# An attention layer gated by an FFN on one core: rotary tables kept on chip, one copy of the keys, query jobs per head, heads that take turns

## What is computed

```python
xn = _layernorm(x)
# attention: H=16 heads, NOPE=128, ROPE=64, VD=128, LORA=64
q = (xn @ wq).reshape(b, s, H, 192).transpose(0, 2, 1, 3)
q_nope, q_pe = q[..., :128], q[..., 128:]
kva = xn @ wkv_a;  ckv, k_pe = kva[..., :64], kva[..., 64:]
ckv = ckv * rsqrt(mean(ckv * ckv) + EPS) * kv_norm_scale
k_nope, v = split((ckv @ wkv_b).reshape(b, s, H, 256)...)
q_pe, k_pe = _rope(q_pe, cos, sin), _rope(k_pe, cos, sin)
scores = (q_nope . k_nope + q_pe . k_pe) * 192 ** -0.5    # causal
out = softmax(scores) @ v;   s = out.reshape(b, s, H * 128) @ wo
# FFN: hidden 704
g = silu((silu(xn @ gate_w.T * gate_s) * (xn @ up_w.T * up_s)) @ down_w.T * down_s)
return x + s * g
```

## Time and profile before

| | before |
|---|---|
| runs | 1116.97, 1118.76, 1122.3 us |
| profiled execution | 1120.68 us, its span 1118.9 us |
| TensorE busy | 985.6 us, 88% (10576 matmuls), mean granted clock 0.95 |
| DVE / ACT / GpSimd busy | 831.2 / 714.0 / 662.8 us |
| DMA | 184.92 MB, mean 165 GB/s; SP's queue q1 has 89.6% of 16 engines' span |
| chain that ended last | TensorE 34%, DMA 24%, DVE 17%, GpSimd 10%, SP queue 6%, ACT 5% |

### The profile page before, as it was taken

How to read it: one execution, slowest core, us unless ns; L and a number is a source line. 1 busy time by engine, 2 the same in 40 slices (tenths; PEclk the granted TensorE clock), 3 DMA queues, 4 the chain that set the end, 5 groups by cost and what they waited for, 6 DMA issues and landing times.

```text
span 1118.9 us, 26420 instructions
## 1 busy us (share of the span) xinstructions
PE 985.6 (88%) x10576; PEld 842.8 (75%) x10576; DVE 831.2 (74%) x1359; ACT 714.0 (64%) x1033; POOL 662.8 (59%) x448
## 2 busy tenths in 40 slices
PE   6864898989988988999889998998899986989998
PEld 5743787778777877788778877876688775878887
DVE  6674687988787877878798779887888885873134
ACT  1335567776676767677677677776677774863232
POOL 3736766766576675756685658565857684422331
PEclk7777899999999999899999999999999998999999
DMA  5118899999999999999999999999999899992001
GB/s 146 38 40 168 152 186 197 197 197 184 184 187 199 189 187 185 202 184 188 189 207 185 197 190 206 180 192 178 202 178 211 179 192 207 178 176 76 1 20 57
DMA packets 600042, 184.92 MB, mean 165 GB/s; under 512 B 574960, under 2 KB 586864, under 8 KB 599920
## 3 DMA queue, kind: packets, MB, share of 16 engines
q1 hardware_dynamic: 595440, 182.57, 89.6%
...
## 4 chain that ended last, share of the span: by engine, by line
PE 34%; DMA 24%; DVE 17%; POOL 10%; SPq 6%; ACT 5%; issue 4%; ACTq 1%; POOLq 0%
DMA pT<-hl 19%; PE s_ps L637 12%; PE s_ps L535 9%; DVE hl L948 5%; PE slot_ps L535 5%; DVE part_max L939 5%; POOL hl L1099 5%; ACT hl L743 3%; DMA sinT<-sinT_dram 2%; SPq L464 2%; ACT prob L809 2%; PE o_ps L653 2%; SPq L477 2%; PE o_ps L535 2%; PE o_ps L654 2%
## 5 line engine op out<-in xcount | busy, mean ns | idle before, releaser
L1099 POOL TENSOR_TENSOR hl<-prob,hl 128x1024 f16<-128x1024 f32 x128 | 274.5, 2144 | 228.3 <-ACT hl L743 224.4
L743 ACT ACTIVATE hl<-prob 128x1024 f16<-128x1024 f32 (+7 forms) x384 | 295.9, 804 | 160.3 <-DMA pT<-hl 159.6
L809 ACT ACTIVATE prob<-s_ps,neg_max 128x1024 f32<-128x1024 f32 (+7 forms) x384 | 316.7, 859 | 101.4 <-DVE neg_max L942 46.6
L939 DVE TENSOR_REDUCE part_max<-s_ps 128x1 f32<-128x1024 f32 (+7 forms) x256 | 243.7, 985 | 93.4 <-PE s_ps L637 74.4
L948 DVE TENSOR_TENSOR hl<-prob,hl 128x1024 f16<-128x1024 f32 (+7 forms) x256 | 255.9, 1035 | 62.4 <-ACT hl L743 62.1
L653 PE MATMUL o_ps<-v,pT 128*128 128x65 f16 x2176 | 231.8, 194 | 51.0 <-DMA pT<-hl 39.3
L653 PEld LDWEIGHTS o_ps<-v,pT 128*128 128x128 f16 x2176 | 205.4, 97 | 58.0 <-DMA pT<-hl 45.9
L654 PE MATMUL o_ps<-v,pT 128*128 128x64 f16 x2176 | 232.2, 196 | 0.0
L655 PE MATMUL o_ps<-v,pT 128*128 128x65 f16 x2176 | 231.1, 193 | 0.0
L655 PEld LDWEIGHTS o_ps<-v,pT 128*128 128x128 f16 x2176 | 205.6, 100 | 0.0
L654 PEld LDWEIGHTS o_ps<-v,pT 128*128 128x128 f16 x2176 | 204.8, 98 | 0.0
...
## 6 DMA issues: line engine op xcount, KB each, us to landing
...
q_swap<-q_pe SPq DMA_DIRECT2D x128, 64.0 KB, 2.1
pT<-hl SPq DMA_TRANSPOSE x256, 5.2
...
```

Of the source, the lines that this page charges most:

```text
L743: return nc.scalar.activation(dst, src, ACT.Copy)
L809: nc.scalar.activation(prob_of(u, m), score_bank(u, m), ACT.Exp, bias=neg_max[:, r:r + 1]).then_inc(exp_done, 1)
L939: nc.vector.tensor_reduce(part_max[:, u % 2, m:m + 1], src, AX.X, ALU.max).then_inc(part_done, 1)
L1099: return lambda: nc.gpsimd.tensor_tensor(dst, a, b, op)
```

## The change

1. **Tables.** `cosT` and `sinT` hold all 2048 columns and are loaded once, in the setup, group by group (8 loads in place of 64). `TABLES_AT` and its waits are gone.
2. **One copy of the keys.** Both heads keep rotary rows at partitions 0 to 63, latent rows at 64 to 127. `KB` and its four setup jobs, ACT copies and DVE subtractions are gone.
3. **Query jobs per head.** `qA{g}` and `qB{g}` make all 128 rows of one head. Each has two ACT copies over 64 rows (into `q_pe` and into the query) and one DVE subtraction. The swap waits for `qB{g}`. Head B's sum now moves from partitions 64 to 127 down to 0 to 63: DVE does it (`rope_of_b`, into `pe_b`), GpSimd only head A's.
4. **Heads take turns.** Unit u is head u % 2, and two units in a row have the same tiles. Groups 3 and 0 are due at units 0 and 1 of a pair, groups 2 and 1 at units 8 and 9; the job and step tables are rewritten for it. `o_pair` becomes two buffers of four tiles, the output jobs come sooner and five, not nine, are left for the FFN stage. The FFN loads move from unit 5 to 6, their first use from unit 6 to 8.

The swap is made by four DMAs before and after; only its place moves.

```diff
-    k = u % HALF
+    k = step_of(u)
-    return u // HALF % 2
+    return u % 2
-    k = u % HALF
+    k = step_of(u)
...
-               ("wkvT", 0), ("xT", 3, 0), ("xT", 3, 1), ("pe3", 0), ("kv", 2), ("wabs", 0), ("kv", 3), ("K", 0, "B"), ("K", 0, "A"),
-               ("pe0", 0), ("lat3", 0), ("K", 1, "B"), ("K", 1, "A"), ("lat0", 0), ("K", 2, "B"), ("K", 2, "A"),
-               ("K", 3, "B"), ("K", 3, "A")]
+               ("wkvT", 0), ("xT", 3, 0), ("xT", 3, 1), ("kv", 2), ("wabs", 0), ("kv", 3), ("qA3", 0), ("qB3", 0), ("K", 0), ("K", 1),
+               ("qA0", 0), ("K", 2), ("qB0", 0), ("K", 3)]
...
-JOBS_NEXT = {2: ["wqT"], 5: ["pe3"], 7: ["wkvT"], 8: ["pe0"], 9: ["wabs"], 11: ["pe2", "lat3"], 12: ["lat0"], 13: ["pe1"],
+JOBS_BEFORE = {2: ["outT3"], 4: ["outP3a", "outP3b"]}
+JOBS_OWN = {0: ["qA2"], 1: ["qB2"], 2: ["qA1"], 3: ["qB1"], 5: ["wvo"], 6: ["outT0"], 7: ["outP0a", "outP0b"], 10: ["outT1"],
+            12: ["outP1a", "outP1b"], 14: ["outT2"], 15: ["outP2a", "outP2b"]}
+JOBS_NEXT = {3: ["wqT"], 5: ["wkvT"], 6: ["wabs"], 8: ["qA3"], 9: ["qB3"], 10: ["qA0"], 11: ["qB0"]}
+FFN_COUNT = {8: 1, 9: 2, 10: 1, 11: 2, 13: 2, 14: 1, 15: 2}
+OUT_LAST = [(name, PAIRS - 1) for name in ("outP2a", "outP2b", "outT3", "outP3a", "outP3b")]
...
+POOL_NEXT = {1: ["wkvs"], 6: ["wpe_hi"], 7: ["wpe_lo"], 10: rope(3)[:1], 11: rope(3)[1:] + ["A3hi"], 12: ["A3lo", rope(0)[0], "B3hi"],
+             13: ["B3lo"] + rope(0)[1:], 14: side("A", 0), 15: side("B", 0)}
+POOL_OWN = {2: rope(2)[:1], 3: rope(2)[1:] + ["A2hi"], 4: ["A2lo", rope(1)[0], "B2hi"], 5: ["B2lo"] + rope(1)[1:], 6: side("A", 1),
+            7: side("B", 1)}
+POOL_FFN = {6: ["up_zero", "up_scale_zero", "down_zero"], 8: ["up_scaled0", "up_scaled1"], 9: ["down_scaled"]}
+ROPE_B_OWN, ROPE_B_NEXT = {4: 2, 6: 1}, {12: 3, 14: 0}
...
-    return scores_through((pair - 1) * PU + head * HALF + (HALF // 2 if g in (3, 0) else HALF) - 1)
+    return scores_through((pair - 1) * PU + (PU // 2 if g in (3, 0) else PU) - 2 + head)
...
-        cosT = ab("cosT", [P, BANK])
-        sinT = ab("sinT", [P, BANK])
+        cosT = ab("cosT", [P, S])
+        sinT = ab("sinT", [P, S])
+        pe_b = ab("pe_b", [LORA, 2, BANK])
...
-            def load_tables(g, pair):
-                n = group_no(g, pair)
-                if n >= 1:
-                    before = GROUP_ORDER[(n - 1) % NG], (n - 1) // NG
-                    sp.wait_ge(pool_done, POOL.after((f"rope{before[0]}.1", before[1])))
-                sp.dma_start(cosT[:], cosT_in[:, query_cols(g)]).then_inc(tables_loaded, 16)
-                sp.dma_start(sinT[:], sinT_in[:, query_cols(g)]).then_inc(tables_loaded, 16)
+            def load_tables(g):
+                sp.dma_start(cosT[:, query_cols(g)], cosT_in[:, query_cols(g)]).then_inc(tables_loaded[g], 16)
+                sp.dma_start(sinT[:, query_cols(g)], sinT_in[:, query_cols(g)]).then_inc(tables_loaded[g], 16)
             def swap(g, pair):
                 half = ROPE // 2
-                sp.wait_ge(act_freed, after("act", (f"pe{g}", pair)))
+                sp.wait_ge(hi_done, after("hi", (f"qB{g}", pair)))
                 n = group_no(g, pair)
                 if n >= 1:
                     before = GROUP_ORDER[(n - 1) % NG], (n - 1) // NG
                     sp.wait_ge(pool_done, POOL.after((f"rope{before[0]}.2", before[1])))
+                    sp.wait_ge(rope_b, n)
                 for i in range(4):
...
-                if u in TABLES_AT:
-                    load_tables(*TABLES_AT[u])
                 turn_rest(u)
...
-                if pair == PAIRS - 1 and k == 5:
+                if pair == PAIRS - 1 and k == 6:
                     load_ffn()
...
-                elif name.startswith("lat"):
+                else:
+                    h, g = "AB".index(name[1]), int(name[2])
                     pe_eng.wait_ge(dve_freed, after("dve", ("wabs", pair)))
-                    c = query_cols(int(name[3:]))
-                    last = exact(ps, [(wabs_hi[:, k, :], wabs_lo[:, k, :], xT_hi[:, k, c], xT_lo[:, k, c]) for k in range(KE)])
-                else:
-                    g = int(name[2:])
                     pe_eng.wait_ge(pool_done, POOL.after(("wpe_lo", pair)))
                     if pair == 0:
                         pe_eng.wait_ge(dve_freed, after("dve", ("xT", g, KE - 1)))
                     c = query_cols(g)
-                    last = exact(ps, [(wpe_hi[:, k, :, :].rearrange("p h c -> p (h c)"), wpe_lo[:, k, :, :].rearrange("p h c -> p (h c)"),
-                                       xT_hi[:, k, c], xT_lo[:, k, c]) for k in range(KE)])
+                    last = exact(ps, [(wc_hi[:, k, h, :], wc_lo[:, k, h, :], xT_hi[:, k, c], xT_lo[:, k, c]) for k in range(KE)])
...
                 elif name == "wabs":
-                    copy(wabs_hi[:].rearrange("p k c -> p (k c)"), ps[:, 0:KE * P]).then_inc(hi_done, 1)
-                elif name.startswith("lat"):
-                    g = int(name[3:])
-                    c = query_cols(g)
-                    if pair > 0:
-                        act.wait_ge(scores_ready, queries_free(1, g, pair))
-                    copy(QA_hi[LORA:P, c], ps[LORA:P, :])
-                    copy(QB_hi[0:LORA, c], ps[0:LORA, :]).then_inc(hi_done, 1)
-                else:
-                    n = group_no(int(name[2:]), pair)
+                    copy(wc_hi[:, :, :, ROPE:P], ps[:, 0:KE * P].rearrange("p (k h c) -> p k h c", k=KE, h=2)).then_inc(hi_done, 1)
+                else:
+                    h, g = "AB".index(name[1]), int(name[2])
+                    n = group_no(g, pair)
                     if n >= 1:
                         before = GROUP_ORDER[(n - 1) % NG], (n - 1) // NG
                         act.wait_ge(swapped, 64 * n)
                         act.wait_ge(pool_done, POOL.after((f"rope{before[0]}.0", before[1])))
-                    copy(q_pe[:], ps).then_inc(act_freed, 1)
+                    copy(q_pe[h * ROPE:(h + 1) * ROPE, :], ps[0:ROPE, :])
+                    if pair > 0:
+                        act.wait_ge(scores_ready, queries_free(h, g, pair))
+                    copy(queries(Q_hi, h, g)[ROPE:P, :], ps[ROPE:P, :]).then_inc(hi_done, 1)
...
+            def query_lo(name):
+                h, g = "AB".index(name[0][1]), int(name[0][2])
+                dve.wait_ge(hi_done, after("hi", name))
+                nc.vector.tensor_tensor(queries(Q_lo, h, g)[ROPE:P, :], slot_bank(name)[ROPE:P, :], f32(queries(Q_hi, h, g)[ROPE:P, :]),
+                                        ALU.subtract).then_inc(dve_freed, 1)
+            def rope_of_b(g, pair):
+                n = group_no(g, pair)
+                dve.wait_ge(pool_done, POOL.after((f"rope{g}.1", pair)))
+                if n >= 2:
+                    before = GROUP_ORDER[(n - 2) % NG], (n - 2) // NG
...
+                    pair, k = divmod(u, PU)
+                    if k in ROPE_B_OWN:
+                        rope_of_b(ROPE_B_OWN[k], pair)
+                    if k in ROPE_B_NEXT and pair < PAIRS - 1:
+                        rope_of_b(ROPE_B_NEXT[k], pair + 1)
...
-                    run((name, pair), tt(turned, q_pe[:], cosT[:], ALU.mult), (act_freed, after("act", (f"pe{g}", pair))),
-                        (tables_loaded, 32 * (n + 1)), *done)
+                    run((name, pair), tt(turned, q_pe[:], cosT[:, query_cols(g)], ALU.mult), (hi_done, after("hi", (f"qB{g}", pair))),
+                        (tables_loaded[g], 32), *done)
                 elif i == 1:
-                    run((name, pair), tt(q_swap[:], q_swap[:], sinT[:], ALU.mult), (swapped, 64 * (n + 1)))
-                else:
-                    run((name, pair), tt(turned, turned, q_swap[:], ALU.add))
+                    run((name, pair), tt(q_swap[:], q_swap[:], sinT[:, query_cols(g)], ALU.mult), (swapped, 64 * (n + 1)))
+                else:
+                    run((name, pair), tt(turned[0:ROPE, :], turned[0:ROPE, :], q_swap[0:ROPE, :], ALU.add))
...
-                rows = slice(head * LORA, (head + 1) * LORA)
-                c = query_cols(g)
-                src = pe[rows, group_no(g, pair) % 2, :]
+                n = group_no(g, pair)
+                src = (pe_b if head else pe)[0:ROPE, n % 2, :]
+                hi, lo = queries(Q_hi, head, g)[0:ROPE, :], queries(Q_lo, head, g)[0:ROPE, :]
                 if name.endswith("hi"):
                     free = ((scores_ready, queries_free(head, g, pair)),) if pair > 0 else ()
-                    run((name, pair), tt(Q_hi[head][rows, c], src, ones[rows, :].to_broadcast([LORA, BANK]), ALU.mult), *free)
-                else:
-                    run((name, pair), tt(Q_lo[head][rows, c], src, Q_hi[head][rows, c].bitcast(F32), ALU.subtract))
+                    added = ((rope_b, n + 1),) if head else ()
+                    run((name, pair), tt(hi, src, ones[0:ROPE, :].to_broadcast([ROPE, BANK]), ALU.mult), *free, *added)
+                else:
```

(1 more changed line is left out.)

184 lines of the change are left out of this document (82 added, 102 removed).

## The result

The changed kernel took **1130.0 us** (median of 9 runs, 1123.84 to 1134.51) against 1117.99 us for the kernel before on the same chip (9 runs). The ratio is 1.010, with a 95% interval of 1.007 to 1.013: slower by 1.0%, where 1063 us had been forecast.

The account below looks back on a forecast made before the run. SyncE's late, full queue of transposes, table loads and swaps was taken as the bound. Middle pairs -38, first pair -14, setup +3, last pair -5, tail -2 sum to -56 us: 1063 us from 1118.8, range 1040 to 1095.

Parts of the forecast that it names:

- Tables: Six middle pairs: dropping the table reloads frees SyncE's queue, 7 us a pair, with ends of 5.8 and 10.9.
- The rival that they were hidden: Middle pairs: table loads cost nothing there, so only the other stages gain; 12 to 15 us, about 1105 us; chance 0.08.
- Setup: Before unit 0: four key jobs fewer but a longer chain of waits; 3 us later, between 3 sooner and 6 later.
- First pair: First pair: becomes a middle pair of 108.1 us plus about 3 until buffers fill; 14 us less (5 to 20).
- What the new order costs there: Middle pairs: added ACT and DVE work covered by queue time, longer swap waits; 0.7 us a pair, ends 0 and 3.
- signs of being wrong: Pairs over 111 us with queue idle and ACT awaiting a maximum; `q_pe` high among waits; first score after 75 us.
- The copy behind the swap: Middle pairs: ACT's copy into `q_pe` follows its awaited swap by one unit; charged within 0.7 us a pair.
- The slower rival: The copy behind the swap becomes the bound, 15 places; 1188 us at worst, 1138 with ACT's waits alone; chance 0.05.
- `rope_of_b`: Middle pairs: DVE's sum for head B, 0.68 us each, 2.7 a pair, covered by queue time; holding GpSimd charged nothing.
- The last pair: Last pair's 15 units: 104.9 us become 99.7, so 5 us less (0 to 9).
- The tail: FFN stage: four of nine output jobs leave it; 2 us less.
- The first rival: Middle pairs: engines behind the queue bite, a pair stops at 111.5 us; 28 us gained, 1091 us; chance 0.24.

Follow-up runs that it names:

- experiment 4: The kernel before, with one group's rope tables loaded once and used for all groups, reloads left out: 1066.06 us, 0.947 of before.
- experiment 1: The changed kernel with two buffers for `q_pe`, so ACT's copy waits for the swap of two groups before: 1094.92 us, 0.973 of the kernel before.
- experiment 2: The changed kernel without DVE's sum for head B in pairs 1 to 7: 1103.69 us, 0.982 of the kernel before.
- experiment 5: The changed kernel with two buffers for `q_pe` and without DVE's sum for head B in pairs 1 to 7: 1072.29 us, 0.956 of before.
- experiment 6: The changed kernel with two `q_pe` buffers and GpSimd's query splits on 8 of 512 columns from pair 1 on: 1067.86 us, 0.952 of before.
- experiment 7: The changed kernel with two `q_pe` buffers and GpSimd's query splits replaced by memsets from pair 1 on: 1070.58 us, 0.952 of before.
- experiment 8: The changed kernel with two `q_pe` buffers and DVE's sum for head B done twice from pair 1 on: 1145.15 us, 1.017 of before.
- experiment 12: The changed kernel, two `q_pe` buffers, head B's sum on GpSimd, its high part moved by DMA ahead of the unit's first transpose: 1081.15 us, 0.961 of before.

## Why the prediction was wrong

**Tables: right.** -7 a pair was forecast, -7.2 measured (experiment 4). The rival that they were hidden is refuted. The Trainium skill (DMA: Bandwidth & Descriptors, Latency and other measured facts) gives DMA transposes 261 GB/s, from which that rival followed; by it, as an estimate, a unit's two transposes need 4.3 us, and the trace has 5.35 us of queue for them. One reading behind it was not good: the DMA share was taken for "no idle time", and over the six middle pairs it is 1.07 with the tables and 1.07 without, at 7.2 us a pair less. It was the late queue that told the bound.

**Setup: right within its ends** (+5.2). The first score matmul starts at 72.49 us. Its size is not sharper than some 5 us: with the same setup jobs, experiments 1, 2 and 5 to 8 reach unit 0 at 80.4 to 85.4.

**First pair: the number right (-12.5), the reason not.** It was to become a middle pair and 3 us; it takes 4.4 us less than a middle pair. And 10.1 us come off with the tables alone, in the old order (experiment 4). That is luck.

**The step that failed** is "What the new order costs there": 0.7 us a pair with 3 as the high end, and engines "covered by the queue's time". With the tables gone the queue's time was the cover that went. Middle pairs came out 9.0 us a pair worse than forecast, and two terms hold 8.2 of them. Of the signs of being wrong that it named two came: `q_pe` high among the waits, and a maximum as what ACT waits for.

The two terms:

- *The copy behind the swap*, charged inside the 0.7: about 5.3 us a pair (117.1 to 111.8, experiment 1). The slower rival had this mechanism, its 15 places (14 seen) and a chain of 7.2 us from low half to landed swap; the trace has 571.35 - 564.32 = 7.0. Its counter-argument was false: ACT was taken to reach the copy a unit, 7 us, after that half, and it reaches it 3.9 us after (568.23), since in its own program only three exponentials, a high half and a copy come between. That leaves 3.1 us, not nothing, bare.
- *`rope_of_b`*, charged nothing: another 3.0 us a pair (111.8 to 108.8, experiment 5), 4.4 where it is taken out first (117.1 to 112.6, experiment 2). It was costed at 0.68 us from a row in the setup and takes 1.12, because it is often held behind a GpSimd step, and it is paid because ACT waits for DVE's maxima. 1.7 to 2.8 points. The sharing of the read interface was looked for in one direction only, DVE holding GpSimd (rows of unit 0, at 79 us, not of unit 66's neighbours); the rows of experiments 2 and 6 show the other.

What is left, 0.7 us a pair over the forecast and 1.6 over experiment 4, holds ACT's second copy per job, the heads' turns and the splits. The second copy was sized right: 0.59 us over 64 rows, as over 128 rows, and ACT is busy 85.9 us a pair where 86 were forecast. DVE's subtractions grew as well, from 1035 to 1132 ns or 24 us in sum, but that is no term of its own in the miss: experiment 5 has them at 1184 ns with a pair of 108.8 us, and experiment 12 at 1207.

**Neither term alone makes the kernel slower**: without the one it stands at 0.973, without the other at 0.982. The slower rival said that its wait decides from 3.7 us bare per place; it had 3.1 in 14 places.

**The last pair** gained nothing (+0.5, forecast -5, 0 to 9 less). GpSimd still waits 6.0 us for the FFN loads, where 1.5 were forecast. Neither of the two terms holds it back: its 15 units take 106.6 us with two buffers, 104.4 without the sum and 104.9 with both removed, against 101.0 in experiment 4. What does stays open. **The tail** gave 0.5 us of 2.

**Chances.** 0.05 for slower was too low by the profile alone: the rival's two prices, 11.3 us of chain and 7 us of slack, both rested on the bound that the change removes, and should have been worked out again at the new pace, engine by engine in program order. The rival itself got its 0.05 at the lateness of a queue that the change took away. The first rival, engines behind the queue, had the right cause. Its 111.5 us a pair was assumed, not worked out; that two buffers give 111.8 is luck.

What stays open: what the 0.8 points between experiments 4 and 5 are made of within each stage, what holds the last pair, how experiment 6's gain divides between DVE and GpSimd, and how much of each price is TensorE's clock. With two buffers, for one, TensorE is busy 614.1 us in the middle pairs at 0.99, in the changed kernel 625.6 at 0.97.
